# Four 32-row tiles for the score products of a decoder layer, and a count taken by ScalarE

## The reference

```python
# self attention, H = 16 heads of 32, per batch
q, k, v = heads(x @ Wq + bq), heads(x @ Wk + bk), heads(x @ Wv + bv)
scores = einsum('bhqd,bhkd->bhqk', q / |q|, k / |k|) / temp   # temp = sigmoid(mean(x) @ Wt + bt) + 0.5
vals, idx = top_k(scores, S // 4)                             # the 64 largest of each row of 256
attn = zeros.at[idx].set(softmax(vals))
out = (attn @ v) @ Wo + bo
gate = sigmoid(x @ Wg + bg)
x = layernorm(x + gate * out + (1 - gate) * x)
x = layernorm(x + cross_attention(x, ctx))                    # one head of 512, ctx 256 wide
x = layernorm(x + sum_k weights[k] * (x @ W[ids[k]].T + b[ids[k]]))   # 8 adapters of 32
```

## Time and profile before

| | |
|---|---|
| time, median of 3 runs | 4504.08 us (4502.92 to 4505.82) |
| profiled execution: from first to last instruction | 4502.0 us |
| time around the span | 2.1 us, median less span |
| PE / DVE / POOL / ACT busy | 79% / 71% / 58% / 51% |
| TensorE's granted clock, mean | 0.858 of full |
| DMA | 17 GB/s over the span |

### The profile page before, as it was taken

One profiled execution on the slowest core, in us unless ns is written; L12 is line 12 of the kernel. 1 busy time (PEld: TensorE's weight loads), 2 busy tenths in 40 slices (PEclk: granted clock), 3 DMA queues, 4 the chain that ended last, 5 costly groups with the idle time before them and its releaser, 6 DMA issues. The chain is left out here.

```text
span 4502.0 us, 63085 instructions
## 1 busy us (share of the span) xinstructions
PE 3540.2 (79%) x16410; PEld 2084.6 (46%) x16410; DVE 3187.3 (71%) x11357; ACT 2315.2 (51%) x5394; POOL 2628.9 (58%) x5061
## 2 busy tenths in 40 slices
PE   3788878778878788887888878888887878887855
PEld 2354444444444444444444444444444444444432
DVE  3677767777767866767777767777767777777772
ACT  1555555554555555554554555554555554555531
POOL 1566665656565656665655665656665656655632
PEclk7898988888988888988898988888888888888877
DMA  4000000000000000000000000000000000000000
GB/s 155 6 13 13 16 14 10 17 17 13 17 12 10 17 17 13 17 12 10 17 17 13 13 17 10 17 17 13 17 13 10 17 17 13 17 13 10 12 13 12
DMA packets 43223, 78.44 MB, mean 17 GB/s; under 512 B 3692, under 2 KB 11884, under 8 KB 42758
## 3 DMA queue, kind: packets, MB, share of 16 engines
q1 hardware_dynamic: 41254, 68.75, 4.6%
q0 software_dynamic: 1504, 5.77, 0.3%
HBM read 57.73 MB, written 16.78 MB: 17 GB/s over the span
## 5 line engine op out<-in xcount | busy, mean ns | idle before, releaser
L1362 DVE SCALAR_TENSOR_TENSOR near<-near,side_guess 128x256 f32<-128x256 f32 x1024 | 476.0, 526 | 480.5 <-POOL near L445 480.5
L1417 DVE SCALAR_TENSOR_TENSOR probs<-scores,threshold,probs 128x256 f32<-128x256 f32 x1013 | 466.4, 513 | 372.4 <-issue 372.4
L456 POOL TENSOR_SCALAR probs<-probs,kept_inv 128x256 f32<-128x256 f32 x1024 | 558.1, 559 | 163.3 <-DVE kept_inv L1445 163.2
L683 ACT ACTIVATE probsT<-turn_ps 128x512 f32<-128x512 f32 x512 | 288.3, 595 | 571.6 <-PE turn_ps L879 570.2
L1030 PE MATMUL score_ps<-kT,qT 128*128 128x256 f32 x2048 | 566.3, 425 | 11.8 <-DVE unsure_n L1405 11.8
L436 POOL TENSOR_SCALAR two_below<-sign_sum 128x4 f32<-128x4 f32 x256 | 62.7, 245 | 820.1 <-ACT near L672 820.1
L672 ACT ACTIVATE near<-scores,neg_guess 128x256 f32<-128x256 f32 x1024 | 507.2, 512 | 29.9 <-POOL neg_guess L427 28.3
L445 POOL TENSOR_SCALAR near<-scores,side 128x256 f32<-128x256 f32 x1024 | 520.5, 524 | 0.0
L879 PE MATMUL turn_ps<-ident,probs 128*128 128x128 f32 x2072 | 348.6, 319 | 189.7 <-POOL probs L456 171.3
L1030 PEld LDWEIGHTS score_ps<-kT,qT 128*128 128x128 f32 x2048 | 421.1, 214 | 122.5 <-issue 46.9
L1376 DVE MATCH_REPLACE8 near<-nearest,near 128x256 f32<-128x256 f32 x1024 | 406.9, 407 | 0.0
(11 more groups left out here) (173 smaller groups left out, 7276.4 us busy)
## 6 DMA issues: line engine op xcount, KB each, us to landing
x_in<-in_x_dram SPq DMA_DIRECT2D x32, 512.0 KB, 3.4
x_res<-in_x_dram SPq DMA_DIRECT2D x32, 512.0 KB, 3.5
out_dram<-rows SPq DMA_DIRECT2D x32, 512.0 KB, 3.4
x_in<-in_ctx_dram SPq DMA_DIRECT2D x32, 256.0 KB, 3.5
scores<-in_L_ffn_W_dram SPq DMA_DIRECT2D x4, 1024.0 KB, 5.5
near<-in_L_ffn_W_dram SPq DMA_DIRECT2D x4, 1024.0 KB, 5.5
w_q<-in_L_attn_Wq_dram POOLq DMA_DIRECT2D x1, 1024.0 KB, 10.4
probs<-in_L_xattn_Wq_dram SPq DMA_DIRECT2D x1, 1024.0 KB, 10.3
```

Of the source, the lines that this page charges most:

```text
L456: pool.tensor_scalar(probs[:, s % 4, j], probs[:, s % 4, j], kept_inv[:, s % 2, j:j + 1], 1.0, ALU.mult, ALU.mult).then_inc(s_pr, 1)
L1362: return [step.mark(dve.scalar_tensor_tensor(out=near[:, r, j], in0=near[:, r, j], scalar=side_guess[:, r, j:j + 1], in1=near[:, r, j], op ...
L1417: step.mark(dve.scalar_tensor_tensor(out=probs[:, s % 4, j], in0=scores[:, s % 4, j], scalar=threshold[:, r, j:j + 1], in1=probs[:, s % 4, ...
```

## The change

- `make_scores` multiplies over 32 rows: for head j it takes partitions 32j to 32j+31 of `qT` and `kT`. `qT` has no zero-padded copies any more; it shrinks to [128, 4, 256], its memset goes, and ACT copies it with one 128x512 instruction in place of four 32x512.
- `score_ps` is laid out by head: [128, 4 heads, 2 buffers, 256], so each head has a bank, and both buffers of a head are in the same bank. `make_scores(s)` therefore waits until `exps(s-1)` has read the other buffer.
- `count_unsure` writes into T[1], the bank of the second half of `turn_probs`, whose second half waits until the count has been taken.
- `take_unsure` moves from DVE to ACT, as one copy with an accumulator for the sum. The counts are kept as float32, and DVE loads their bits as integers: above zero is above zero.
- In stage 6, PE's `count_unsure(i, 5)` moves from ahead of `key_moments(nxt)` and `row_moments(nxt)` to behind them, since these use T[1]; ACT takes it after its own `row_moments(nxt)`.

```diff
-        qT = sb("qT", [P, HQ, G, S])
+        qT = sb("qT", [P, G, S])
-        unsure_n = sb("unsure_n", [1, 2, HQ + 1], I32)
+        unsure_n = sb("unsure_n", [1, 2, HQ + 1])
-        score_ps = ... [P, 2, HQ, S]
+        score_ps = ... [P, HQ, 2, S]
-                pool.memset(qT[:], 0.0).then_inc(s_const, 1)
 # ACT, front_turn
-                for j in range(HQ):
-                    own = slice(j * DH, j * DH + DH)
-                    last = act.activation(qT[own, j, :, part], T[0][own].rearrange("p (g k) -> p g k", g=G),
-                                          ACT.Copy)
-                last.then_inc(s_qkt, 1)
+                act.activation(qT[:, :, part], T[0][:].rearrange("p (g k) -> p g k", g=G), ACT.Copy)\
+                   .then_inc(s_qkt, 1)
 # ACT, new; in stage s of the body ahead of take_probs, behind cross_exp (s = 5) and row_moments (s = 6)
+            def take_unsure(b, s):
+                act.wait_ge(s_fl_f, at(b, NQ, s + 1))
+                act.activation(unsure_n[:, s % 2, 0:HQ], T[1][0:1, 0:HQ], ACT.Copy,
+                               accum_out=unsure_n[:, s % 2, HQ:HQ + 1]).then_inc(s_fl, 1)
 # PE
             def make_scores(b, s):
-                if s >= 3:
-                    pe.wait_ge(s_fl, at(b, NQ, s - 2))
...
+                if s or not (isinstance(b, int) and b == 0):
+                    pe.wait_ge(s_ex, at(b, NQ, s))
                 for j in range(HQ):
-                    mm = pe.matmul(score_ps[:, s % 2, j], qT[:, j, g, t * P:t * P + P], kT[:, g],
+                    own = slice(j * DH, j * DH + DH)
+                    mm = pe.matmul(score_ps[:, j, s % 2], qT[own, g, t * P:t * P + P], kT[own, g],
                                    start=True, stop=True)
             def count_unsure(b, s):
                 pe.wait_ge(s_bad, at(b, NQ, s + 1))
-                if s < NQ - 1:
-                    pe.wait_ge(s_ex, at(b, NQ, s + 2))
...
-                pe.matmul(score_ps[0:1, (s + 1) % 2, 0, 0:HQ], ones[:, 0:1], unsure[:, s % 2],
+                if s or not (isinstance(b, int) and b == 0):
+                    pe.wait_ge(s_fl, at(b, NQ, s))
+                pe.matmul(T[1][0:1, 0:HQ], ones[:, 0:1], unsure[:, s % 2],
                           start=True, stop=True).then_inc(s_fl_f, 1)
             def turn_probs(b, s):
                 for half in range(2):
                     pe.wait_ge(s_pr, at(b, NQ * HQ, s * HQ + 2 * half + 2))
+                    if half and not (isinstance(b, int) and b == B - 1 and s == NQ - 1):
+                        pe.wait_ge(s_fl, at(b, NQ, s + 2))
 # PE, stage 6 of the body
-                count_unsure(i, 5)
                 if not last:
                     key_moments(nxt)
                     row_moments(i, nxt, first)
                     pe.wait_ge(s_mu, at(nxt, 1, 1))
+                count_unsure(i, 5)
                 turn_probs(i, 4)
 # DVE: take_unsure goes, keep_top loads the bits
-            def take_unsure(b, s):
-                dve.wait_ge(s_fl_f, at(b, NQ, s + 1))
...
-                    dve.tensor_copy(unsure_n[:, s % 2, 0:HQ], counts)
-                    dve.tensor_reduce(unsure_n[:, s % 2, HQ:HQ + 1], counts, AX.X, ALU.add).then_inc(s_fl, 1)
-                n = dve.value_load(unsure_n[0:1, r, HQ:HQ + 1], min_val=0, max_val=P * HQ)
+                n = dve.value_load(unsure_n[0:1, r, HQ:HQ + 1].bitcast(I32), min_val=0, max_val=MOST)
```

More of the change, by code:

```diff
@@ L16 @@
 SCALE = 0.25
+MOST = 0x7F000000
 QUANTILE = 0.695
@@ L285, in decoder_layer @@
         s_seq_v = sem("vector_wait_carriers")
-        NCONST = 11
+        NCONST = 10
         def att_bank(s):
@@ L653, in copy_scores @@
                     act.wait_ge(s_inv, at(b - 1, NQ, NQ + s - 3))
-                act.activation(scores[:, s % 4], score_ps[:, s % 2], ACT.Copy).then_inc(s_sc, 1)
+                act.activation(scores[:, s % 4], score_ps[:, :, s % 2], ACT.Copy).then_inc(s_sc, 1)
             def exps(b, s):
-                act.activation(probs[:, s % 4], score_ps[:, s % 2], ACT.Exp, scale=1.0 / SCALE).then_inc(s_ex, 1)
+                act.activation(probs[:, s % 4], score_ps[:, :, s % 2], ACT.Exp, scale=1.0 / SCALE).then_inc(s_ex, 1)
             def signs(b, s):
@@ L779, in body @@
                         row_moments(nxt)
+                    if s or not first:
+                        take_unsure(*((i, s - 1) if s else (prev, NQ - 1)))
                     if s >= 2 or not first:
@@ L857, in _ @@
             body(B - 1, False, True)
+            take_unsure(B - 1, NQ - 1)
             for s in (NQ - 2, NQ - 1):
@@ L1029, in make_scores, with count_unsure @@
                 for j in range(HQ):
-                    mm = pe.matmul(score_ps[:, s % 2, j], qT[:, j, g, t * P:t * P + P], kT[:, g],
+                    own = slice(j * DH, j * DH + DH)
+                    mm = pe.matmul(score_ps[:, j, s % 2], qT[own, g, t * P:t * P + P], kT[own, g],
                                    start=True, stop=True)
                 mm.then_inc(s_sc_f, 1)
-            def count_unsure(b, s, i=None):
+            def count_unsure(b, s):
                 pe.wait_ge(s_bad, at(b, NQ, s + 1))
-                if s < NQ - 1:
-                    pe.wait_ge(s_ex, at(b, NQ, s + 2))
-                elif i is not None:
-                    pe.wait_ge(s_ex, at(i, NQ, 1))
-                pe.matmul(score_ps[0:1, (s + 1) % 2, 0, 0:HQ], ones[:, 0:1], unsure[:, s % 2],
+                if s or not (isinstance(b, int) and b == 0):
+                    pe.wait_ge(s_fl, at(b, NQ, s))
+                pe.matmul(T[1][0:1, 0:HQ], ones[:, 0:1], unsure[:, s % 2],
                           start=True, stop=True).then_inc(s_fl_f, 1)
@@ L1112, in body @@
                 if not first:
-                    count_unsure(prev, NQ - 1, i)
+                    count_unsure(prev, NQ - 1)
                     turn_probs(prev, NQ - 2)
@@ L1271, in _ @@
             for s in (NQ - 2, NQ - 1):
+                if s == NQ - 1:
+                    pe.wait_ge(s_pt, at(z, 2 * NQ, 2 * NQ - 2))
                 turn_probs(z, s)
@@ L1398, in set_threshold @@
                 return step.mark(dve.tensor_tensor(threshold[:, r], part_sum[:, 0], part_sum[:, 1], ALU.add))
-            def take_unsure(b, s):
-                dve.wait_ge(s_fl_f, at(b, NQ, s + 1))
-                with nc.allow_low_precision(reason="a count of at most 512, exact"):
-                    counts = score_ps[0:1, (s + 1) % 2, 0, 0:HQ]
-                    dve.tensor_copy(unsure_n[:, s % 2, 0:HQ], counts)
-                    dve.tensor_reduce(unsure_n[:, s % 2, HQ:HQ + 1], counts, AX.X, ALU.add).then_inc(s_fl, 1)
             def keep_top(b, s):
@@ L1497, in body @@
                     found = search(i, s, masked)
-                    if s or not first:
-                        take_unsure(*back)
                     if s == 3 and not first:
@@ L1535, in _ @@
             step.restart()
-            take_unsure(B - 1, NQ - 1)
             keep_top(B - 1, NQ - 1)
```

4 lines of the change are left out of this document (2 added, 2 removed).

## The result

The changed kernel takes 4274.2 us (4273.36 to 4282.45) against 4503.97 us, a ratio of 0.949 with a 95% interval of 0.948 to 0.951: 230 us gained where I had summed 80. Its profiled execution spans 4272.9 us.

A forecast was written before the change was run, and what follows sets the result against it. A loop through several engines was taken to set the time. Quiet batches gain 3.0 us each (21: -63), nine others -9, first and last -8: span 4502.0 - 80 = 4422, median 4424 us; range 4310 to 4480.

The forecast's parts named there:

- The keep steps' 1.28 us: DVE before its keep steps: the bare load, compare and branch of the count would be hidden behind the search.
- Rival 3: Score products: row tiles don't run side by side, 2.2 us a batch lost again, 4470 us; chance 0.10.
- The 2.3 us "stay": DVE before stage 1's keep step: a further 2.3 us, taken as instruction fetching behind the branch, would remain.
- (b): DVE from stage 1's mask to `mean_var` of stage 3: gains of 1.6, 1.4 and 0.13 us, reaching -4.1.
- rival 1: DVE's 2.3 us of fetching move from stage 1 to a stage off the path: 4380 us; chance 0.25.
- The half clock of cross-attention "stays": PE's cross-attention products in the quiet batch: idle time ahead stays some 5 us, so they keep running at half clock.
- (c): From `mean_var` through POOL's norm1, `pick_side(4)`, `scale_probs(2)` to PE's turn: shift -4.1 us, PE's idle time some 5 us.
- The moved count "eats 4.0 us": Stage 5's count behind the moments: `keep_top(5)` and `query_moments` wait for it on the path, costing 4.0 us.
- (e): ACT's q and k copies through row moments (L645) to DVE's `query_moments`: -2.8 us from copies, `query_moments` at -4.2.
- a term sized 2.4: First ffn product: after 5.4 us of PE idling it runs at slower clock, about 6.1 us, costing 2.43.
- rival 4: PE's longer wait before `turn_probs(prev, 7)` slows the clock for projections behind it: slower than before, 4540 us; chance 0.08.
- The nine other batches "-9": Batches with the slow keep step on the path and ffn already slow: each gains 1.0 us, -9 in all.

The follow-up runs named there:

- f2: Changed kernel with 45 one-column memsets in VectorE's setup, shifting its loop code: 4299.7 us.
- f1: Kernel before with 64 one-column memsets in VectorE's setup, shifting its loop code: 4493.5 us.
- a1: Kernel before with only ScalarE as taker of the counts, the count's product in its old place: 4233.3 us.
- u1: Changed kernel with score products over 128 rows and four zero-padded q copies again, PSUM layout and count as changed: 4327.9 us.
- c3: Kernel before with eight unread products ahead of `turn_probs(2)` in stage 4: 4420.6 us.
- v1: Changed kernel with the count of stage 5 ahead of the key moments again, in the other accumulator bank, taken by ScalarE: 4288.8 us.
- a2: As a1, with the count of stage 5 moved behind the key and row moments: 4316.1 us.
- c1: Changed kernel with five unread products in stage 0, ahead of `turn_probs(prev, 7)`: 4234.9 us.
- v5: Changed kernel with early count of stage 5, score products over 128 rows, four padded q copies and five unread products in stage 0: 4249.3 us.
- u2: Changed kernel with q copied by four 32-row instructions in place of one: 4281.1 us.
- v6: Changed kernel with early count of stage 5 and unread products in stage 0, ahead of ffn and ahead of `turn_probs(2)`: 4152.9 us.

## Why the prediction was wrong

**What held.** Score products: 0.74 us for 0.76 said. The keep steps' 1.28 us: gone in stages 1, 2, 4, 7, by the sequencer running ahead. In stage 0, where I said the same, it is not: there the count comes last, and the step starts 1.27 us behind it, which costs nothing, as the shift stays at the -1.2 us that the mask before it has. `mask(1)`: -1.2 for -1.0. L991's wait: 1.25 for 1.3. Stage 6's keep step stands for the count, and the query moments start right behind it. The take costs 0.24 us where I took 0.35. Rival 3 is out. The Trainium skill (TensorE: Matmul & The Clock Gate, Part 3) measured 3.07 times for four row tiles of 512 columns; here, with 256 columns and up to the next product, it is 1.93 to 0.74, or 2.6 times, and the measured number stands.

**The 2.3 us "stay".** Failed step: (b), -1.6 in stage 1; it was -3.9. I let the sequencer run ahead for the load and branch and left the 2.3 us, which I took for the fetch, bare behind them. Nothing of them is seen any more: the count lies ready 5.5 us early, room for both. The changed time is also free of it in f2, at another code position, so cover is the likelier account than rival 1's luck of position, though no run separates cover from absence outright. f1 tells only that it can move, not what its absence alone would be worth.

**The half clock of cross-attention "stays".** Failed step: (c), "its idle time stays some 5 us". POOL's probs came 5.6 us earlier in the batch (61.2 to 55.6 us after `make_scores(nxt, 1)`), TensorE's `make_scores(5)` only 0.8 (54.0 to 53.2), since w_k had become slow. So the idle time in `turn_probs(2)` fell from 4.0 to 1.9 us in the median, and in 11 of 26 batches the product took 3.7 us: its end is at -7.1 where I had -4.1. The idle time doesn't tell which: it is 1.7 to 2.2 us ahead of products of 3.7 us and of those of 5.4 and more. With products over 128 rows (a1, u1) TensorE has no idle time there, and all 26 are fast. c3 gives the price, 2.6 us.

**The moved count "eats 4.0 us".** Failed step: (e), the path through L645 and `query_moments`. I saw DVE wait there 3.19 us and took that for the path, and never looked at whether POOL, which takes the result, was free. It took the moments up 0.94 us after they were ready even before, and 2.44 us after in the quiet batch of the changed kernel. The path into the guesses runs `cross_add`, `mean_var`, norm 2, `pick_side`, `scale_probs`; the count's wait is hidden beside it (v1), unless the keep step comes so late that `scale_probs`, which needs it, is late as well (a2, in part of its 83 us).

**The clock elsewhere.** ffn takes 5.4 us in the median, not 6.1: a term sized 2.4 that measured 1.7. And what rival 4 says came true at the place I named, w_k after `turn_probs(prev, 7)`. TensorE's wait there grew from 1.29 to 2.78 us in the batch shown, and the product takes 5.5 us, at a smaller price than I gave it: DVE's mask of stage 2 has 3.5 us of the 5.1 that keep step 1 had, and c1 puts the loss at 39 us, with what cross-attention has of it. I had it at 8% as a loss of its own; it should have been a term of the sum. The shortened scores are not its only cause: in u1 and a2, with products over 128 rows, the wait in both halves of that turn is 1.6 and 1.5 us in the median, as in the kernel before (1.5), and w_k is slow all the same.

**The nine other batches "-9".** This term failed as well: they gave 68 us, 7.6 each, about as much as the quiet ones with 7.3. I had let them gain only 1.0 each, since their slow keep step lies on the path. Of the 149 us that my sum misses, 90 are in the quiet batches and 59 in these. What shortens them I did not trace batch by batch.

**The sum as it measured** (medians of the 26 batches): -5.1 at keep step 1; 1.6 back ahead of mask 2, while w_k is slow; -1.2 at keep step 2; 1.1 back ahead of mask 3, which now waits for POOL; -1.3 in stage 3, where that mask is shorter; so -4.8 at `mean_var`, rounded. Then -0.6 to the cross-attention product and -1.6 in it; 1.0 back up to the guesses; -1.6 to ffn, ScalarE being free earlier; +1.7 in ffn; -0.3. Together -6.3.

**Whose gain it is.** The runs make a chain from before to the changed kernel, one part at a time: ScalarE's take -271 (a1), the late count +83 (a2), the bank layout with the counts in T[1] +12 (u1), the tiles -47 (u2), the single copy -7; together -230. So more than the whole comes from the count's move. The layout cost 29 us in v5, with the early count and the unread products; why, I did not separate. And TensorE's clock sits in each of these numbers: tiles bring the idle time ahead of cross-attention, the single copy that ahead of ffn (slow in 28 of 64 products with it, in 2 to 5 in a1, a2, u1 and u2). What unread products win back at w_k and ffn (39 and 45 us) is no price of the tiles alone.

## What to carry to other kernels

A value that a sequencer must load before it branches is best made by another engine, early: here the load, the branch and what lay behind them vanished under running work. Work taken off TensorE becomes idle time somewhere, and the next product may pay for it at half clock; look at the products behind each wait that will grow, and price them in the sum. When a wait seems to set the path, look at what the engine that takes the result was doing at that moment.

## What the runs showed of the hardware

Products whose results nobody reads can pay: v6 differs from v1 in nothing but 17 of them a batch and a semaphore wait ahead of eight, and takes 4152.9 us where v1 takes 4288.8. Four VectorE masks of 128x256 took 3.06 us in stage 3 of before, beside POOL's `scale_probs` and norm 1, and 1.67 us in the changed kernel, beside POOL's small operations; this was not tested by itself. The same ffn product of 8 records took 3.70 us behind a wait of 1.91 us (u2) and 5.17 us behind one of 4.23 us (the changed kernel), while cross-attention came out slow and fast behind the same 1.7 to 2.2 us. And the changed kernel takes 25 us longer with 45 memsets ahead of the loop, for a reason that no row shows, so a difference of that size between two versions need not come from what was changed in them.
